# Pages of padding, the first loads and the last tiles rearranged in an attention and expert kernel, with half the GpSimd sets among its scatters

## The reference

```python
x = x + attention(layernorm(x), ctx, ctx, lens2, Wq, Wk, Wv, Wo)   # 16 heads of 16, keys past lens2 masked
u = layernorm(x)
s = softmax(u @ centroids.T + expert_biases)          # 16 experts
topk_vals, topk_idx = top_k(s, 2)
routed = sum over the two of topk_vals * (u @ Wr[e].T + br[e])
shared = (sum over 2 of u @ Ws[n].T + sum(bs)) / 2
x = x + u + routed + shared
```

## Time and profile before

| | us |
|---|---|
| median of 3 runs | 264.41 |
| lowest and highest | 262.88, 266.91 |
| the profiled execution | 264.64 |
| its span, first to last instruction | 262.7 |

### The profile page before, as it was taken

The page is one execution under the profiler, slowest core; times in us unless marked ns, Lnnn a source line. Parts: engine busy times, 40 slices in busy tenths (PEclk is TensorE's granted clock), DMA queues, the critical chain, the costliest instruction groups (busy, mean ns, idle before and its releaser), DMA issues.

```text
span 262.7 us, 5125 instructions
## 1 busy us (share of the span) xinstructions
PE 220.6 (84%) x1543; PEld 185.1 (70%) x1543; DVE 161.0 (61%) x508; ACT 96.0 (37%) x241; POOL 136.9 (52%) x235
## 2 busy tenths in 40 slices
PE   7958999999889998889899697798959798846394
PEld 3837888798878888779888476586737686625283
DVE  2799678888878889888885556176613242230261
ACT  3113566655546556555444220223213232210022
POOL 1440221435645556545586742088888888885000
PEclk9999999999889999999999979799997999999689
DMA  5989999999511022112121321567677511200996
GB/s 168 368 242 218 288 309 326 406 429 412 224 44 41 20 83 85 63 46 75 60 103 60 122 83 49 156 196 233 200 207 218 166 67 37 92 15 3 364 383 208
DMA packets 20314, 45.12 MB, mean 172 GB/s; under 512 B 5283, under 2 KB 13989, under 8 KB 19112
## 3 DMA queue, kind: packets, MB, share of 16 engines
q1 hardware_dynamic: 12624, 27.76, 33.2%
q0 software_dynamic: 5664, 13.03, 13.4%
q10 hardware_dynamic: 2000, 4.01, 4.3%
HBM read 23.22 MB, written 46.29 MB: 265 GB/s over the span
## 4 chain that ended last, share of the span: by engine, by line
PE 66%; DMA 10%; DVE 7%; issue 7%; POOL 4%; SPq 2%; ACT 1%; POOLq 0%; DVEq 0%; ACTq 0%
PE O L923 12%; PE B L882 6%; PE T L845 6%; PE T L1101 5%; PE B L1101 5%; PE S L845 5%; PE S L894 4%; PE A L1101 4%; PE B L996 4%; PE O L1101 4%; PE A L845 3%; DMA lists<-padblock,run_i 3%; DMA ebias<-in_ebias 2%; DVE rowmax L691 2%; DMA wr<-y 2%
## 5 line engine op out<-in xcount | busy, mean ns | idle before, releaser
L547 POOL DMA_INDIRECT lists<-urow,pos x32 | 32.8, 1026 | 41.2 <-PE S L894 31.2
L494 ACT ACTIVATE uTl<-S 128x256 f32<-128x256 f32 x47 | 17.7, 384 | 59.5 <-PE S L845 50.0
L422 ACT ACTIVATE pT<-T 128x512 f32<-128x512 f32 (+1 forms) x48 | 25.3, 526 | 28.3 <-PE T L845 26.3
L923 PEld LDWEIGHTS O<-vfront,pT 128*128 128x128 f32 x256 | 29.9, 192 | 0.3 <-DVE logits L714 0.3
L923 PE MATMUL O<-vfront,pT 128*128 128x34 f32 x256 | 30.1, 273 | 0.0
L845 PE MATMUL T<-const,s_sb 128*128 128x128 f32 (+1 forms) x160 | 25.9, 276 | 3.9 <-DVE s_sb L706 3.1
L691 DVE TENSOR_REDUCE rowmax<-S 128x16 f32<-128x1232 f32 x16 | 23.1, 1442 | 9.3 <-PE S L894 8.1
L448 ACT ACTIVATE urow<-x,shift,rstds 128x256 f32<-128x256 f32 x32 | 19.0, 595 | 13.8 <-POOL shift L561 13.5
L845 PEld LDWEIGHTS T<-const,s_sb 128*128 128x128 f32 (+1 forms) x160 | 19.6, 141 | 6.3 <-issue 4.5
L882 PE MATMUL B<-xT,wqc 128*128 128x128 f32 x128 | 18.3, 286 | 6.5 <-issue 5.0
L590 POOL DMA_INDIRECT y<-yrow,padblock x16 | 15.6, 976 | 12.6 <-DVE yrow L823 10.0
(11 more groups left out here) (203 smaller groups left out, 469.8 us busy)
## 6 DMA issues: line engine op xcount, KB each, us to landing
lists<-padblock SPq DMA_DIRECT2D x3, 2056.0 KB, 19.7
padblock<-lists SPq DMA_DIRECT2D x32, 128.5 KB
wr<-in_wrT SPq DMA_DIRECT2D x1, 4096.0 KB
br<-in_br SPq DMA_DIRECT2D x1, 2048.0 KB
wr<-y SPq DMA_DIRECT2D x4, 512.0 KB, 8.4
wr<-y ACTq DMA_DIRECT2D x4, 512.0 KB, 8.7
urow<-lists SPq DMA_DIRECT2D x15, 128.5 KB
x<-in_x SPq DMA_DIRECT2D x1, 1024.0 KB, 27.7
```

Of the source, the lines that this page charges most:

```text
L422: nc.scalar.activation(pT[t % 2][0:rows, c0:c1, :], T[0:rows, 0:c1 - c0, :], ACT.Exp).then_inc(p_ready, 1)
L494: nc.scalar.activation(uTl[k % NU][:, :, :], flips[k % 4][:, 0:D].rearrange("p (c n) -> p c n", c=DC), ACT.Copy).then_inc(lT_ready, 1)
L547: nc.gpsimd.indirect_dma_start(out=lists, out_offset=bass.IndirectOffsetOnAxis(ap=pos[:, t, c:c + 1], axis=0), in_=urow[t % NR][c][:, :], ...
L923: last = M(to, pT[t % 2][0:v.shape[0], c, :], v.rearrange("p h j -> p (h j)"), start=(c == 0), stop=(c == CH - 1), skip_group_check=True)
```

## The change

Constants and waits:
- REACH 3 becomes 5: five first pages are filled at the start, `pad_page` runs for 11 tiles in place of 13, and tile t waits for page t - 5. Four semaphores (`INFLIGHT`) in place of two allow four pages in flight. `filled` is split: tile 0 waits for two fills, tile 2 for the rest.
- `padblock` is set first of all on GpSimd, in four parts; SP's wait ahead of the fills is for that. The dummy block is filled last. x and xT of tiles 8 to 15 stay behind the fills.

Start: wq ahead of the context on SP, lens ahead of the constants on ScalarE's queue; tile 0's statistics behind the key blocks and tile 2's behind tile 0's scores; the waits for the rest of the constants and for the expert biases move behind tile 0's scores; the value products of batch 1 (`project_front`, `project_rest`) stand behind the output projection and behind the third group of transposes of step 0; the shared weights are made in step 1. The warm-up has 512, 512 and 256 columns.

Drain: on GpSimd page, scatter and 1/std change order; tile 14 is routed in a bank of its own and chosen ahead of tile 15's residual; tile 15 is routed from transposes of x itself (`lastT`) against centred centroids (`centc`), and its logits are multiplied by 1/std at the end; its u is transposed later, for the shared product only.

List stage: two lists are transposed in advance, the next ones follow the first two products; the set on GpSimd stands behind every other scatter.

```diff
-REACH = 3
+REACH = 5
+INFLIGHT = 4
@@ block.sync
-            sp.wait_ge(pool_set, 3)
-            sp.dma_start(lists[DUMMY:DUMMY + P, :], padblock[:, 0, :]).then_inc(filled, 16)
+            sp.wait_ge(pool_set, 2)
             per_expert = lists[0:DUMMY, :].rearrange("(e n) w -> e n w", e=EXPERTS)
             for page_of in range(REACH):
                 sp.dma_start(per_expert[:, page_of * P:(page_of + 1) * P, :].rearrange("e (b r) w -> e b (r w)", r=RUN),
-                             padblock[:, :, :].rearrange("p r w -> p (r w)")).then_inc(filled, 16)
+                             padblock[:, :, :].rearrange("p r w -> p (r w)")).then_inc(filled[int(page_of >= 2)], 16)
+            sp.dma_start(lists[DUMMY:DUMMY + P, :], padblock[:, 0, :]).then_inc(filled[1], 16)
             load_x(sp, 3)
             load_xT(sp, 3)
@@ block.scalar, step TILES
+                if s == TILES:
+                    act.wait_ge(centc_psum, 1)
+                    nc.scalar.activation(centc[:, :, :], idle_bank[:, 0:DC * EXPERTS].rearrange("p (c e) -> p c e", c=DC),
+                                         ACT.Copy).then_inc(centc_ready, 1)
+                    act.wait_ge(uT_psum, t + 1)
+                    nc.scalar.activation(uT[t][:, :, :], u_bank(t), ACT.Copy).then_inc(uT_ready, 1)
+                    row(t, 1).then_inc(row1_ready, 1)
...
+                if s == TILES:
+                    act.wait_ge(lastT_psum, 1)
+                    nc.scalar.activation(lastT[:, :, :], spare, ACT.Copy).then_inc(lastT_ready, 1)
@@ block.gpsimd
+            for j in range(0, RUN, 4):
+                nc.gpsimd.memset(padblock[:, j:j + 4, 0:D], 0.0)
+            nc.gpsimd.memset(padblock[:, :, D:ROW].bitcast(i32), PADROW).then_inc(pool_set, 1)
...
-            nc.gpsimd.memset(padblock[:, :, 0:D], 0.0)
-            nc.gpsimd.memset(padblock[:, :, D:ROW].bitcast(i32), PADROW).then_inc(pool_set, 1)
...
             for s in range(TILES + 3):
-                if s == TILES:
+                if 1 <= s - 4 <= TILES - REACH:
+                    pad_page(s - 4)
+                if TILES - 1 <= s <= TILES:
                     scatter_rows(s - 3, s)
                 if is_tile(s - 1):
                     scale_second(s - 1)
-                if is_tile(s - 3) and s != TILES:
+                if is_tile(s - 3) and not TILES - 1 <= s <= TILES:
                     scatter_rows(s - 3, s)
-                if 1 <= s - 3 <= TILES - REACH:
-                    pad_page(s - 3)
...
-                if k < LISTS - 1:
-                    if k >= 2:
-                        pool.wait_ge(paused, k - 1)
-                    nc.gpsimd.memset(passed_x[:, k % 2, :], 0.0).then_inc(paused, 1)
+                if k % 2 == 1:
+                    if k >= 3:
+                        pool.wait_ge(paused, k // 2)
+                    nc.gpsimd.memset(passed_x[:, 0, :], 0.0).then_inc(paused, 1)
@@ block.vector
+                if t == TILES - 1:
+                    dve.wait_ge(rstds_ready, t + 1)
+                    V.scalar_tensor_tensor(out=logits[:, t, :], in0=O[:, 0:EXPERTS], scalar=rstds[:, t, 0:1], in1=ebias[:, :],
+                                           op0=ALU.mult, op1=ALU.add).then_inc(r_taken, 1)
...
+                if s == TILES:
+                    take_logits(s - 2)
+                    choose(s - 2)
@@ block.tensor, drain
             transpose_u(t - 1)
             pe.wait_ge(p_ready, 3 * TILES)
             rank(t - 2)
             pe.wait_ge(o_ready, TILES)
+            pe.wait_ge(centc_ready, 1)
             for c in range(DC):
                 last = transpose(A[:, c, :], o_sb[t % 2][:, c * P:(c + 1) * P])
             last.then_inc(oT_psum, 1)
...
+            rank(t - 1)
+            pe.wait_ge(out_taken, TILES)
+            for c in range(DC):
+                last = transpose(spare[:, c, :], x[:, t, c * P:(c + 1) * P])
+            last.then_inc(lastT_psum, 1)
+            shared(0)
+            pe.wait_ge(lastT_ready, 1)
+            for c in range(DC):
+                last = M(route_bank(t), lastT[:, c, :], centc[:, c, :], start=(c == 0), stop=(c == DC - 1))
+            last.then_inc(r_psum, 1)
             shared(1)
...
-            for k in range(AHEAD):
+            for k in range(AHEAD - 1):
                 list_transposes(k).then_inc(list_stepped, 1)
...
-                if k + AHEAD < LISTS:
-                    last = list_transposes(k + AHEAD)
+                for j in {0: (AHEAD - 1,), 1: (AHEAD, AHEAD + 1)}.get(k, (k + AHEAD,) if k + AHEAD < LISTS else ()):
+                    last = list_transposes(j)
                 last.then_inc(list_stepped, 1)
```

More of the change, by code:

```diff
@@ L277, in flipped @@
         def flipped(k):
-            return k + 1
+            return k + 1 if k < AHEAD else max(k, AHEAD + 1)
         def multiplied(k):
-            return AHEAD + k + 1
+            return AHEAD + k
         def coming(s):
@@ L467, in _ @@
                 t = s - 2
-                if is_tile(t):
+                if s == TILES + 1:
+                    row(t, 1).then_inc(row1_ready, 1)
+                if is_tile(t) and s != TILES:
                     act.wait_ge(uT_psum, t + 1)
@@ L654, in _ @@
                     cst("headmask").unsqueeze(1).unsqueeze(3).to_broadcast([P, BATCH, 2, NKEYS]), ALU.mult).then_inc(kblock_ready, 1)
-            for t in range(1, FIRST):
+            for t in range(2):
                 ln1(t, mv1[:, t, :])
@@ L722, in _ @@
             V.memset(page[:, 0:1], float((REACH - 1) * PARTS))
-            dve.wait_ge(arrived["rest"], 16)
-            dve.wait_ge(arrived["ebias"], 16)
             for s in range(-1, TILES + 3):
@@ L772, in _ @@
                 t = s - 2
-                if is_tile(t) and not TILES - 2 <= s < TILES:
+                if is_tile(t) and not TILES - 2 <= s <= TILES:
                     take_logits(t)
@@ L776, in _ @@
                     subtract_max(s + 1)
-                if is_tile(t):
-                    dve.wait_ge(r_taken, t + 1)
-                    link(V.max(top8[:, t, :], logits[:, t, :]))
-                    link(V.max_index(idx8[:, :], top8[:, t, :], logits[:, t, :]))
-                    link(V.tensor_tensor(onehot[:, :, :], cst("expert").unsqueeze(1).to_broadcast([P, TOPK, EXPERTS]),
-                                         idx8[:, 0:TOPK].unsqueeze(2).to_broadcast([P, TOPK, EXPERTS]), ALU.is_equal))
-                    V.tensor_tensor(chosen[:, :], onehot[:, 0, :], onehot[:, 1, :], ALU.add).then_inc(chosen_ready, 1)
+                if is_tile(t) and s != TILES:
+                    choose(t)
+                t = s - 3
+                if 1 <= t <= TILES - REACH:
+                    dve.wait_ge(reached_ready, t)
+                    link(V.tensor_scalar(page[:, t:t + 1], reached[:, :], EIGHTS, EIGHTS, ALU.add, ALU.subtract))
+                    link(V.tensor_scalar(dropped[:, :], page[:, t - 1:t], page[:, t:t + 1], BEYOND, ALU.is_equal, ALU.mult))
+                    V.scalar_tensor_tensor(out=run_i[:, t:t + 1], in0=page[:, t:t + 1], scalar=cst("run"), in1=dropped[:, :],
+                                           op0=ALU.add, op1=ALU.add).then_inc(run_ready, 1)
                 if s == -1:
                     value_masks()
+                    ln1(2, mv1[:, 2, :])
                     value_block(0)
                 if s == 0:
+                    value_block(1)
+                    dve.wait_ge(arrived["rest"], 16)
+                    dve.wait_ge(arrived["ebias"], 16)
+                if s == 1:
                     shared_weights()
@@ L847, in _ @@
             pe.wait_ge(warm_set, 1)
-            for _ in range(3):
-                M(T[:, :, :].rearrange("p a n -> p (a n)"), warm[:, 0:P], warm[:, :], start=True, stop=True)
+            for n in (512, 512, 256):
+                M(T[:, :, :].rearrange("p a n -> p (a n)")[:, 0:n], warm[:, 0:P], warm[:, 0:n], start=True, stop=True)
             pe.wait_ge(center_ready, 1)
@@ L1013, in _ @@
                     queries(n)
+                elif s == TILES - 1:
+                    for to in range(DC):
+                        for c in range(DC):
+                            last = M(idle_bank[:, to * EXPERTS:(to + 1) * EXPERTS], center[:, int(c != to), :], cent[:, c, :],
+                                     start=(c == 0), stop=(c == DC - 1))
+                    last.then_inc(centc_psum, 1)
                 else:
@@ L1037, in rank @@
                 M(rank_bank(t), ones16[:, :], seen, start=False, stop=True).then_inc(rank_psum, 1)
-            def route(t):
-                pe.wait_ge(uT_ready, t + 1)
-                if t == TILES - 1:
-                    pe.wait_ge(r_taken, t)
-                for c in range(DC):
-                    last = M(O[:, 0:EXPERTS], uT[t][:, c, :], cent[:, c, :], start=(c == 0), stop=(c == DC - 1))
-                last.then_inc(r_psum, 1)
             t = TILES - 1
@@ L1056, in _ @@
             last.then_inc(oT_psum, 1)
-            pe.wait_ge(wsr_ready, 1)
-            pe.wait_ge(uT_ready, t - 1)
```

(5 more changed lines are left out.)

106 lines of the change are left out of this document (60 added, 46 removed).

## The result

| | before | after |
|---|---|---|
| median of 4 runs each, us | 264.46 | 253.79 |
| lowest and highest | 262.88, 266.91 | 251.44, 258.02 |
| the profiled execution | 264.64 | 252.99 |
| its span | 262.7 | 251.2 |

The ratio is 0.9586, with an interval of 0.9476 to 0.9695: faster by 4.1%; it is taken over fast runs, without the changed kernel's 258.02 us, which fell in the chip's slower state. The forecast was 261.0 us, with a range of 254.5 to 267.0.

The account below looks back on a forecast made before the run. The prediction took TensorE to bound the loop and GpSimd to be steady in the list stage. Fills +3.0 (whatever the start won), drain -4.65 and list stage -1.95 gave -3.6: 264.6 - 3.6 = 261.0 us, range 254.5 to 267.

Parts of the forecast that it names:

- the loop goes by TensorE: Attention loop, 18 to 141 us: TensorE, busy 114.0 of 123.0 us, was taken to set its pace.
- hidden under the same scores: Attention loop: moving VectorE's three small page operations behind the statistics was claimed to be worth nothing.
- The price of five fills: Loop at tile 8: fills at 8.5 us each delay x to 63.9, ScalarE stands 8.1 us, whole loop +3.0 us.
- The start: Before the loop: bias wait, early padblock set and moved value products, less costs, net -2.7 us at step 1.
- The drain: Between loop and lists: tile 15's scatters no longer wait for the last page; list loads 4.65 us earlier.
- the other steps, in the clock of before: Drain: the remaining steps timed at the old profile's clock, giving first list load at 158.3 against 162.95.
- Step (a): Drain: GpSimd sends tile 12's scatters ahead of tile 14's scales, making all of tile 15's output 1.6 us later.
- (b): Drain: tile 15 routed by raw x, scaled by 1/std at the end; positions at 153.2 against 155.28.
- The list stage: Y-row scatters: fewer sets shorten only the last 20 pitches by 0.0975 us each, -1.95 us.
- up to list 26 GpSimd is not what sets the end: List stage: GpSimd had caught up with VectorE, so until there the stage follows the list loads, -4.65 us.
- The clock: Loop: one fall of TensorE's clock counted on either side, so 0, with +1.5 us as the other end.
- signs of being wrong: x landing before 56 or behind 67; list loads under 3 us closer to loop's end; GpSimd awaiting VectorE at list end.

Follow-up runs that it names:

- group 1: Runs on chip X: changed kernel 257.71 us; with page operations put back 258.51; kernel before with them moved behind 259.63; changed kernel with tile 14's scales first 254.64.
- chip Y: One of three chips used for follow-ups; the kernel before took 262.91, 262.95 and 262.83 us there, the changed kernel 246.38 and 247.21.
- group 2: Variants of the changed kernel on chip Y: all sets 251.41 us, no sets 242.18, x and xT ahead of the fills 250.82, REACH = 3 246.62.
- group 4: Runs on chip Y: kernel before 262.72 us; changed kernel 247.21; with constant wr column 247.00; with REACH = 3, no sets and scales first 242.57.
- chip X: One of three chips used for follow-ups; the kernel before took 265.86 us there, the changed kernel 257.71.
- the first variant of group 1: The changed kernel with VectorE's three page operations put back ahead of the residual addition: 258.51 us, ratio 0.9721.
- the second: The kernel before with only VectorE's three page operations moved behind the statistics and the choice of their step: 259.63 us, ratio 0.976.
- group 5: Runs on Z: changed kernel 256.18 us; changed kernel with TensorE's column of wr from a constant, not a register, 256.21 us.
- Z: One of three chips used for follow-ups; the kernel before took 264.67 us there, the changed kernel 256.18.

## Why the prediction missed

**What bounds the loop: the reading failed.** The forecast said "the loop goes by TensorE" from its busy time and took VectorE's page operations as "hidden under the same scores", at 0. The chain of waits was read in the drain and not in a step of the loop; there lines 758 to 760 stand in it by name, 0.56 us a step. A share of 93% left room for exactly this. Ten steps of it are 5.7 us, the largest single term of the first pair, and the kernel before with that edit alone gains 6.2 us (group 1). No rival had it.

**The price of five fills: right in kind, wrong in size and place.** The forecast had x at 63.9 by 8.5 us a fill, and +3.0 us. It landed at 57.2; on chip Y at 13.58 + 40.7 = 54.3. On chip Y the landings of the fills are all known:

```profile
L381 SPq DMA_DIRECT2D lists<-padblock x5: 588/600/659, 9.7 to 12.3; - x5
...
DMA to landing us min/median/max: 13.6/26.7/34.8
```

The first lands at 9.7 + 13.6 = 23.3 and the last at 12.3 + 34.8 = 47.1, so (47.1 - 23.3) / 4 = 5.95 us a fill, not 8.5, and the first 3.6 earlier than forecast. x follows the last fill by 7.2 us, not 3.0: 4.1 of them are the dummy block, which the forecast counted into the first fill, and the rest is as forecast. The 5.95 us are a mean of unequal gaps (7.9, 6.6, 5.6 and 3.7). The step took the two gaps of one profile of before, 8.5 us each, for the rate of the pattern. The chip isn't the reason: the kernel before on chip Y has its fills down at 28.1, 36.9 and 45.0, as in the first profile, and with REACH = 3 in the changed kernel they come at 23.1, 30.8 and 36.6. What in the changed start makes them faster wasn't tried. The Trainium skill ("DMA: Bandwidth & Descriptors", Specifications) has the limit between memory and one core at about 358 GB/s, by which a fill is an estimated 5.9 us; the mean gap agrees, the single gaps and those of before do not, and as a limit it isn't borne out here: all DMAs of the core together moved 433 GB/s from 65 to 70 us (group 2). By the forecast's own sum x costs nothing up to 60.9, and the step around 57.3 is 7.44 us. What the fills did cost was not x: tile 2's scatter took long to land beside the loads that they had pushed back (group 2),

```profile
61.21 14.38 DMA lists<-urow,pos
```

and its buffer is wanted again by ScalarE at 73 (the 2.61 us at 75.68 above). The steps of 8.82 and 7.96 us are +1.9 in place of the +3.0; in six profiles on chip Y with this order of loads they are +0.9 to +2.0. The forecast followed SP's queue as far as x, and not the loads behind x and the engines that these share with the scatters. That the stall is gone with REACH = 3 and 4, and grows with x first, shows that the fills bring it. That they do so by wr and br rests on the landings; and why this scatter took 14 us, where those of tiles 0 and 1 took 7 to 9 beside the same loads, isn't shown.

**The start** was -2.7 and measured -3.57; set, bias wait and scaling behaved as said. On chip Y the pair gives -6.48, of which 2.9 are a fall of the clock in that one execution of before (group 4).

**The drain** was -4.65 to the list loads. It measured 16.31 us from tile 15's division to the first load against 19.34, so -3.03. The step that failed is "the other steps, in the clock of before": the granted clock was 0.50 for the first 10 us of the drain, where before it was 1.00. It cannot be put down to one execution: all profiles of the changed kernel and its variants have such a fall of about 7 or 10 us there, those of the kernel before have the first 7 to 9 us at 1.00. Step (a), forecast at +1.6, measured +2.25 at the residual add (4.81 us behind o_sb against 2.56); the scales came 1.3 later, as the order says, and the output's four matmuls took 0.9 longer. From the add to the positions (b) has 5.1 us and the trace 6.5 (before, 8.8). So the positions of tile 15 come 11.3 us behind o_sb, where they came 11.4 before (155.28 - 143.91), and not 2.1 earlier: (a) and the slow clock ate what the routing by raw x gained. All 3.03 us came from the page wait. What makes the clock fall there isn't shown. The length of the fall goes with that of the drain: with REACH = 5 and this order, division to first load took 15.8 to 17.5 us in seven profiles with some 10 us of it, and 13.8 to 16.0 in five with some 7. The first y scatter followed the load by 6.54 us in place of 7.74, another 1.2 that the forecast did not count; before, the clock had fallen once more in that stretch (0.57 from 166 to 170 us).

**The list stage** was -1.95 and measured +0.74 in the first pair and -3.92 on chip Y. The pitches were forecast right: 1.28 to 1.31 without a set (1.27), 1.46 to 1.48 with one. The failed step is "up to list 26 GpSimd is not what sets the end". GpSimd's waits at 198.31 and 210.53 are pauses of the kind that chip Y does not have: the kernel before there has 46 pitches that are nearly all 1.46 to 1.48. So the rows were those of a disturbance, not of VectorE's own pace. Without pauses half the sets are worth 23 x 0.18 = 4.1 us, over all lists, and with them nothing: with less GpSimd work per list its waits for rows grew by as much. On chip X it is the same: 70.33 us in the old stage with all sets, 71.95, 73.49 and 72.92 in the three kernels with half of them.

**The clock** was set at 0 with 1.5 us as the other end. In the middle of the loop the fall was in each of three profiles of the old kernel's loop (steps of about 8.55 and 9.0, at 64 to 81 or 98 to 116 us) and in none of five profiles of the changed kernel, so the term was -1.6 there; in the drain it was against the change, as told above. The fall is not tied to the place of the page operations: the first variant of group 1 has them in the old place and no such steps, the second has them in the new place and the fall in its last step, and the variant of group 5 without the register load had two steps of 9.73 and 9.57 us, with a granted clock of 0.77 from 62 to 72 us.

**The sum.** On 262.7 of span: -3.57 - 4.67 - 4.23 + 0.74 + 0.23 = -11.50, which is 251.2. Of the signs that the forecast named, those for the first scaling and the missing page in the chain of the drain came out right. The mean of the last twenty pitches was 1.49 us in this profile, not under 1.4; it was 1.385 on chip Y. The gap on ScalarE ahead of tile 8 was 2.6 us at 57, not 5 or more at 64, and "the first y scatter 2 to 3 us earlier" is wrong by 10 us: it came 12.5 us earlier. Of the signs of being wrong two were barely missed in this profile (x at 57.2 against 56, the loads 3.03 us closer against 3), and GpSimd waited once for VectorE in the last twenty pitches (0.87 us at 217.0); on chip Y x landed at 54.3, before 56. None of them looked at the steps of the loop.

## What to carry to other kernels

Before an operation is called hidden behind a busy engine, read one period of the loop in the chain of waits: whatever small operation is named there costs its full time in each step. Bulk writes at the head of a queue push back all that stands behind them, and other queues pay as well: here a scatter issued when the writes had been down for 14 us, beside loads that they had delayed. A sum made in the clock of the old profile needs a look at the new one's: a stretch may keep its work and lose its clock, as the drain did. Waits that come at irregular places of a regular stage are not that stage's pace, and a second chip may not have them: a gain that a kernel can show may hang on that (here half the sets were worth 3.9 us on one chip and nothing on others).

## What was not expected of the hardware

The same changed kernel took 246.4 and 247.2 us on chip Y, 257.7 on X and 256.2 on Z, while the kernel before took 262.7 to 263.0, 265.9 and 264.7: the chips differ by 4 to 5% for one kernel and by about 1% for the other. On X and Z ScalarE and VectorE stand up to 3.4 us for a signal of TensorE where ScalarE stands 0.7 on Y, and register loads have no part in it. A scatter of 128 rows lands in 2.9 us in the median and took 14.4 us beside the loads that five fills had pushed back. Two executions of one kernel may differ by a fall of the granted clock to 0.50 for some 7 us: the kernel before had one at 17 to 23 us on chip Y and none there in the first profile, worth 2.9 us. A set of 256 columns between GpSimd's scatters, 0.33 us long, costs 0.18 to 0.19 us of pitch, since the idle time ahead of the next scatter shrinks from 0.30 to 0.17.
